# Edge network of a graph kernel: the table stands in the array and the one-hot moves, in two column tiles

## The chip, the cores and the metric

The kernel runs on one NeuronCore of one Trainium2 chip. Its engines are TensorE (PE: matmuls, with its weight loads shown as PEld), VectorE (DVE), ScalarE (ACT), GpSimd (POOL) and SyncE (SP, which here starts DMAs). The time of a run is the device time of the core in microseconds (us); the smaller the better.

## What is computed

Four graph layers run one after the other on 12500 nodes and 412500 edges (sorted by target). The change is in the third layer, a message passing network with 64 features and two rounds. Its edge part, cut to what matters:

```python
def _mlp(x, w0, b0, w1, b1):
    return silu(x @ w0 + b0) @ w1 + b1
...
for s in range(2):
    inp = concatenate([e, n[senders], n[receivers]], -1)
    upd_e = _ln(_mlp(inp, edge_blk_w0[s], edge_blk_b0[s], edge_blk_w1[s], edge_blk_b1[s]), ...)
    e = e + upd_e
    agg = segment_sum(upd_e or e, receivers, N)
    ...
```

The kernel multiplies each node's features by its share of edge_blk_w0 before the edges are visited, so the first layer of an edge is: a row picked from the sender table, plus a row picked from the receiver table, plus the edge's own state times its weights. The change is in how these rows are picked and added.

## The kernel before, in words

The two rounds are two edge passes, "first pass" (sorted_mlp with rnd 0, enc true, which also encodes the edge attributes) and "second pass" (rnd 1). In the trace both have tiles called e_s_...; the first pass lies at 8100 to 13790 us of the profiled execution, the second at 14200 to 18080.

The edges lie in 110 blocks of 35 cells of 128 slots. Cells 0 to 32 hold edges whose sender lies in a chunk of the table known beforehand (three chunks of 128 rows for each cell, all kept in SBUF as three bf16 parts in `parts`), cell 33 edges whose sender lies in the block's window, cell 34 the rest ("spill"), whose sender rows POOL fetches with an indirect DMA. Every cell also picks its receiver's row from the window. A block is worked in five groups of cells, PARTS5: 8, 8, 8, 8 and 3.

For each group and block:
- DVE `picks` (L1927, L1928) makes one-hots in bf16: `pick` (128 table rows by 128 slots for each chunk and cell) and `to_hot` for the window.
- PE `gather` (L2289 to L2294) loads a one-hot of 128 columns and moves 64 columns of the table through it, 9 matmuls a cell and 3 more for the window, into a bank `ps_g` with slots as partitions.
- DVE `gathered_` (L1944 to L1948) copies the bank to `g_sb` and adds the spill rows.
- PE `hidden1` (L2309) transposes `g_sb` by pairs of cells into the bank `ps_h1` (two cells of 64 features as partitions) and adds the edge state times weights there (L2312 in the first pass, L2315 in the second).
- ACT `act1_` (L2152) takes the bank through Silu; PE `out1` (L2322, L2325) is the second layer; ACT `out1_` (L2165, L2169) copies its result and squares it; DVE `var1` sums the squares.

Once a block DVE's `roots` (from L2036, twelve small steps) gives the standard deviations of both norms. Then `norm1` scales, and PE adds the messages up (`sums` L2352 in the first pass; `part0`, `less0`, `part1`, `part2` and `part_sums` L2341 in the second). The first pass also encodes the next block: `hidden0` (L2243), `act0_`, `out0` (L2250, L2253), `out0_` (copy and square), `var0`, `norm0` (L1935), and turns the states with `first_` (L2263) and `second_` (L2272). The attributes are turned by `attr_` (L2232).

Each engine has its own queue, written out by hand and strict in order; semaphores tie them. `body(k, x, before)` is one trip: it encodes block k, picks and computes block k - 1, and sums block k - 2, in steps s. On PE (L2364) a step of the first pass holds, in this order: first_(s-1), gather(s), hidden0(s), second_(s-1), sums(s-1), out0(s-1), hidden1(s-2), out1(s-3); after the steps comes carry. In the second pass: gather(s), part_sums(s-3), hidden1(s-2), out1(s-3). On ACT (L2182) a step holds: keep_first(s-2), keep_second(s-2), widens(s), part0(s-1), part1(s-2), first_(s-1), act0_(s), second_(s-1), out0_(s-1), act1_(s-2), out1_(s-3), each where the pass has it. DVE's body (L2039) ends with var0(4), windows, picks(0), picks(1) of the next block, the variances and roots.

In the first pass there is one bank each for ps_g, ps_h1 and ps_o1 (all eight banks are in use), in the second two of each. SP loads the states of a group after the hidden1 two groups back (L1860).

## Time and profile before

| | us |
|---|---|
| median of 3 runs (20420.85 to 20447.48) | 20424.32 |
| the profiled execution's own time | 20439.97 |
| its span, first to last instruction | 20438.1 |
| PE busy | 15983.6 (78%) |
| DVE busy | 13947.1 (68%) |
| ACT busy | 8065.7 (39%) |
| mean granted TensorE clock | 0.810 |

The busy time of each engine in 40 slices of 511 us shows the passes (each digit is tenths):

```profile
PE   2666667666668995999999999985999999966665
DVE  3777777777757995555454555545777777769999
ACT  1444444444432332555555555542333333321111
PEclk9555555655557996999999999997999999977676
```

Slices 16 to 27 are the first edge pass, 28 to 36 the second. In a timeline a row gives the start, the length to the end of the last instruction in it, the instructions merged, and in brackets how long the engine stood idle before it and for whom. Matmuls are pipelined: the time that one takes from the engine is from start to start, not its length. An f32 matmul runs as two records of two passes each. A row of the busy times of a stretch gives from and to, the length, the busy us (and instructions) of PE, PEld, DVE, ACT and POOL, the granted clock, the DMA share and GB/s. A row of a group by line gives line, engine, operation, out<-in, the shapes of the array and the operand, the count | busy us, mean ns of one | idle us of the engine before them and who ended it.

### The profile page before, as it was taken

To read this page: it belongs to the slowest core of one execution; us is meant where nothing else is said; L and a number is where in the kernel's file an instruction comes from. 1 tells how busy PE (TensorE), PEld (TensorE's weight loads), DVE (VectorE), ACT (ScalarE), POOL (GpSimd) and SP (SyncE) were. 2 spreads that over 40 slices of the span, in tenths; PEclk is the share of its full clock that TensorE was granted. 3 is DMA by queue.
4 is the path that set the end of the run, shared out by engine and by line. 5 is a ranking of instruction groups with operands and counts; after the bars stand their busy time and mean duration, and the time that the engine had idled before them with its cause. 6 is when DMAs were issued, how large, how long until landed. Compare 5 with 4: busy or idle time off the path is not lost. (4 is left out here: it accounts for less than half of the span.)

```text
span 20438.1 us, 578367 instructions
## 1 busy us (share of the span) xinstructions
PE 15983.6 (78%) x212634; PEld 14313.7 (70%) x212634; DVE 13947.1 (68%) x33417; ACT 8065.7 (39%) x17256; POOL 5201.9 (25%) x3993
## 2 busy tenths in 40 slices
PE   2666667666668995999999999985999999966665
PEld 1666666666656994888888888884777777756665
DVE  3777777777757995555454555545777777769999
ACT  1444444444432332555555555542333333321111
POOL 1888888888850110000000000000000000001111
PEclk9555555655557996999999999997999999977676
DMA  1222222222223551333333333322555555526666
GB/s 55 54 55 54 53 53 53 53 53 53 54 47 109 158 156 55 106 109 108 109 108 107 109 108 109 107 99 89 156 158 156 157 156 155 156 72 195 184 200 183
DMA packets 1482421, 2200.00 MB, mean 108 GB/s; under 512 B 773752, under 2 KB 960902, under 8 KB 1438482
## 3 DMA queue, kind: packets, MB, share of 16 engines
q1 hardware_dynamic: 1168298, 1839.20, 28.9%
q0 software_dynamic: 139040, 67.50, 3.8%
q10 hardware_dynamic: 173744, 272.32, 3.6%
q8 instruction: 1222, 20.02, 0.4%
q14 instruction: 117, 0.96, 0.0%
HBM read 1651.47 MB, written 523.16 MB: 106 GB/s over the span
## 5 line engine op out<-in xcount | busy, mean ns | idle before, releaser
L764 POOL DMA_INDIRECT records<-e_sort_rec,e_sort_index x3300 | 4339.2, 1315 | 1064.6 <-issue 990.2
L2289 PE MATMUL e_s_ps_g<-e_s_parts,e_s_pick 128*128 128x64 bf16 x65340 | 2900.2, 199 | 700.8 <-DVE e_s_to_hot L1928 336.8
L2289 PEld LDWEIGHTS e_s_ps_g<-e_s_parts,e_s_pick 128*128 128x128 bf16 x65340 | 2658.8, 102 | 849.6 <-issue 507.8
L2400 POOL DMA_INDIRECT e_s_spill<-send,e_s_lists x220 | 227.0, 1032 | 10094.0 <-DVE e_s_g_sb L1948 5471.4
L2294 PE MATMUL e_s_ps_g<-e_s_window,e_s_to_hot 128*128 128x64 bf16 x23100 | 1971.1, 199 | 0.0
L1944 DVE COPY e_s_g_sb<-e_s_ps_g 128x512 f32<-128x512 f32 x880 | 607.1, 690 | 1982.7 <-PE e_s_ps_h L2312 1376.6
L1093 PE MATMUL e_sort_acc<-e_sort_thirds,e_sort_hot 128*128 128x48 f32 x7260 | 1574.8, 414 | 318.6 <-DVE e_sort_hot L923 318.6
L1093 PEld LDWEIGHTS e_sort_acc<-e_sort_thirds,e_sort_hot 128*128 128x128 f32 x7260 | 1557.1, 332 | 351.0 <-DVE e_sort_hot L923 351.0
L2152 ACT ACTIVATE e_s_act<-e_s_ps_h,col_state 128x512 f32<-128x512 f32 (+1 forms) x1100 | 706.9, 643 | 1444.9 <-PE e_s_ps_h L2315 1390.3
L2294 PEld LDWEIGHTS e_s_ps_g<-e_s_window,e_s_to_hot 128*128 128x128 bf16 x23100 | 1263.6, 102 | 0.0
L1927 DVE TENSOR_SCALAR e_s_pick<-e_s_rows,lane_below 128x1024 bf16<-128x1024 bf16 (+1 forms) x3300 | 1244.6, 434 | 0.0
L2325 PEld LDWEIGHTS e_s_ps_o<-w_eblk,e_s_act 128*128 128x128 f32 x7920 | 1041.5, 192 | 259.1 <-issue 218.7
L1010 ACT ACTIVATE e_sort_away<-iota,e_sort_slots 128x128 f32<-128x128 f32 x3850 | 1171.0, 388 | 10.7
L1072 PE MATMUL e_sort_y<-e_sort_window,e_sort_turned 128*125 128x128 f32 x6600 | 1058.2, 330 | 58.0 <-DVE e_sort_prod L890 50.2
L1072 PEld LDWEIGHTS e_sort_y<-e_sort_window,e_sort_turned 128*125 128x125 f32 x6600 | 989.4, 236 | 115.0 <-DVE e_sort_prod L890 76.9
L2325 PE MATMUL e_s_ps_o<-w_eblk,e_s_act 128*128 128x128 f32 x7920 | 1061.7, 275 | 0.0
L1982 DVE TENSOR_REDUCE e_s_stat<-e_s_sq 128x8 f32<-128x512 f32 (+1 forms) x1100 | 652.6, 617 | 490.5 <-ACT e_s_sq L2169 490.4
L979 ACT ACTIVATE e_sort_turned<-e_sort_turn 128x500 f32<-128x500 f32 x880 | 493.7, 561 | 1181.1 <-PE e_sort_turn L1058 1023.8
L2352 PE MATMUL e_s_ps_sum<-e_s_unit,e_s_wide 128*128 128x128 f32 x7700 | 951.2, 275 | 0.1
L2315 PE MATMUL e_s_ps_h<-e_s_states,w_states 128*128 128x512 f32 x2200 | 941.2, 550 | 0.0
L1058 PE MATMUL e_sort_turn<-ident,e_sort_hot_d 125*128 125x125 bf16 x3300 | 502.7, 304 | 527.1 <-ACT e_sort_turned L979 449.4
L1344 PE MATMUL e_s_g<-e_s_parts,e_s_pick 128*128 128x48 bf16 x21780 | 815.2, 206 | 119.6 <-DVE e_s_pick_own L1240 64.4
(542 smaller groups left out, 35650.4 us busy)
## 6 DMA issues: line engine op xcount, KB each, us to landing
e_s_rows<-rows_d SPq DMA_DIRECT2D x330, 1088.0 KB, 5.3
e_s_hot<-hots_d SPq DMA_DIRECT2D x550, 560.0 KB, 4.1
e_s_states<-states SPq DMA_DIRECT2D x880, 256.0 KB, 3.7
e_s_to_rows<-rows_d SPq DMA_DIRECT2D x220, 608.0 KB, 6.0
e_s_rows<-rows_d SPq DMA_DIRECT2D x220, 544.0 KB, 4.9
e_s_rows<-rows_d SPq DMA_DIRECT2D x220, 512.0 KB, 5.5
e_s_to_rows<-rows_d SPq DMA_DIRECT2D x220, 512.0 KB, 6.5
states<-e_s_first_t ACTq DMA_DIRECT2D x440, 256.0 KB, 2.0
```

The lines of the kernel that those rows point to most:

```text
L764: pool.indirect_dma_start(records, bass.IndirectOffsetOnAxis(ap=index[x][:, t:t + 1], axis=0), rec[x][:, t, :], None,).then_inc(written[x] ...
L1010: last = act.activation(away[:, n - c, :], iota128[:, :], ACT.Square, scale=-1.0, bias=slots[x][:, n, 1:2])
L1072: mm = pe.matmul(ps_y[j % 2][0:P, (n - t) * AF:(n - t + 1) * AF], turned[x][:, n, :], window[x][:, :], start=True, stop=True)
L1093: mm = pe.matmul(acc[c // ACC][:, c % ACC * SPAN * F:(c % ACC + 1) * SPAN * F], hot[:, c, :], thirds[:, c, :, :].rearrange("p h f -> p (h ...
L1344: mm = pe.matmul(ps_g[g][:, at:at + 3 * F], pick[x][:, h, c * LANES:(c + 1) * LANES], parts[:, SPAN * c + h, :, :].rearrange("p r f -> p ( ...
L1927: dve.tensor_scalar(pick[p][:, h, 0:(f - c) * LANES], rows_[:, c * LANES:f * LANES], lane_below[:, h:h + 1], None, ALU.is_equal).then_inc( ...
L2152: act.activation(act1[p][:, 0:turned(s)], ps_h1[p % NB][:, 0:turned(s)], ACT.Silu, bias=(col_state if enc else col_state1)[:, :]).then_inc ...
L2289: pe.matmul(to_, pick[p][:, h, here], parts[:, SPAN * c + h, r, :], start=h == 0 and r == 0, stop=False)
L2294: mm = pe.matmul(to_, to_hot[p][:, here], window[:, r, 1, :], start=c == SPILL and r == 0, stop=r == 2)
L2315: mm = pe.matmul(ps_h1[p % NB][:, 0:n_], w_states1[r][:, :], states[p][:, r, 0:n_], start=False, stop=r == 1, skip_group_check=True)
L2325: mm = pe.matmul(ps_o1[p % NB][:, j * LANES:(j + 1) * LANES], act1[p][:, j * LANES:(j + 1) * LANES], W[f"eblk1{rnd}"][:, :], start=False, ...
L2352: mm = pe.matmul(ps_sum[:, 0:2 * D if enc else D], wide[s][:, (c - c0) * LANES:(c - c0 + 1) * LANES], units_of(x, c), start=c == 0, stop=F ...
```

## The change

The roles in the pick are swapped. The table part (128 rows by 64 columns) is loaded as the standing operand, and the one-hot (128 columns) moves. The result has features as partitions, which is the form that the first layer needs, so it goes straight into the bank `ps_h1`: cells of even place in the group into partitions 0 to 63, of odd place into 64 to 127, by two column tiles of the array of 64 columns each. Pick matmuls alternate between the two. The receiver rows of a group are picked with three matmuls for each half, of up to 512 columns. The spill rows are added in hidden1 by a matmul with the identity. The banks ps_g, the copies `gathered_`, the tile g_sb and the transposes are gone; ps_h1 has two banks in the first pass and five in the second. hidden1 comes one group after its gather, not two, and stands in a step right after hidden0; act1_, out1 and out1_ are one step earlier as well. gather waits for act1_ of the group that used its bank before (`aH`). POOL's spill DMA waits for hidden1 of two blocks before.

```diff
+        NH = 2 if enc else 5
...
-        ps_g, ps_h1, ps_o1, ps_sum = ps("g", NB), ps("h1", NB), ps("o1", NB), ps("sum")[0]
+        ps_h1, ps_o1, ps_sum = ps("h1", NH), ps("o1", NB), ps("sum")[0]
+
+        def hidden_bank(x, s):
+            return ps_h1[(x + s) % 2 if enc else s]
...
-            def gathered_(k, x, s, before):
-                p = (x + s) % 2
-                n_ = width(s)
-                dve.wait_ge(tg.sem, tg.at(f"{s}", k))
-                if s >= 2 or before:
-                    dve.wait_ge(tH.sem, group_at(tH, "", k, s, 2))
-                if s < NG - 1:
-                    dve.tensor_copy(g_sb[p][:, 0:n_], ps_g[p % NB][:, 0:n_]).then_inc(vg.sem, 1)
-                else:
-                    dve.tensor_copy(g_sb[p][:, 0:n_ - D], ps_g[p % NB][:, 0:n_ - D]).then_inc(vg.sem, 1)
-                    dve.wait_ge(spilled[x], block_of(k, x, 16))
-                    dve.tensor_tensor(g_sb[p][:, n_ - D:n_], ps_g[p % NB][:, n_ - D:n_], spill[x][:, :], ALU.add).then_inc(vg.sem, 1)
...
-                    if main and s:
-                        gathered_(k - 1, y, s - 1, before - 1)
...
-                act.activation(act1[p][:, 0:turned(s)], ps_h1[p % NB][:, 0:turned(s)], ACT.Silu, bias=(col_state if enc else col_state1)[:, :]).then_inc(aH.sem, 1)
+                act.activation(act1[p][:, 0:turned(s)], hidden_bank(x, s)[:, 0:turned(s)], ACT.Silu, bias=(col_state if enc else col_state1)[:, :]).then_inc(aH.sem, 1)
...
+                    if main and 1 <= s < NG + 1:
+                        act1_(k - 1, y, s - 1, before - 1)
                     if main and 2 <= s < NG + 2:
-                        act1_(k - 1, y, s - 2, before - 1)
-                    if main and s >= 3:
-                        out1_(k - 1, y, s - 3, before - 1)
+                        out1_(k - 1, y, s - 2, before - 1)
 
...
             def gather(k, x, s, before):
                 c0, e = PARTS5[s]
                 p = (x + s) % 2
+                halves = [hidden_bank(x, s)[half * D:(half + 1) * D, :] for half in range(2)]
                 pe.wait_ge(vp.sem, vp.at(f"to{s}", k))
                 if s == 0:
                     pe.wait_ge(vx.sem, vx.end(k))
-                if s >= NB or before:
-                    pe.wait_ge(vg.sem, group_at(vg, "", k, s, NB) if s >= NB or NB - s > 1 else vg.end(k - 1))
-                for c in range(c0, e):
-                    here = slice((c - c0) * LANES, (c - c0 + 1) * LANES)
-                    to_ = ps_g[p % NB][:, (c - c0) * D:(c - c0 + 1) * D]
-                    if c < OWN:
-                        for h in range(SPAN):
-                            for r in range(3):
-                                pe.matmul(to_, pick[p][:, h, here], parts[:, SPAN * c + h, r, :], start=h == 0 and r == 0, stop=False)
-                    elif c == OWN:
+                if s >= NH or before:
+                    pe.wait_ge(aH.sem, group_at(aH, "", k, s, NH))
+                to_pairs = to_hot[p][:, :].rearrange("p (j w l) -> p w j l", w=2, l=LANES)
+                for r in range(3):
+                    for half in range(2):
+                        n_ = (e - c0 + 1 - half) // 2
+                        pe.matmul(halves[half][:, 0:n_ * LANES], window[:, r, 1, :], to_pairs[:, half, 0:n_, :], start=r == 0, stop=False,
+                                  skip_group_check=True)
+                for j in pairs(s):
+                    mine = [(half, c0 + 2 * j + half) for half in range(2) if c0 + 2 * j + half < OWN]
+                    for h in range(SPAN):
                         for r in range(3):
-                            pe.matmul(to_, to_hot[p][:, here], window[:, r, 0, :], start=r == 0, stop=False)
+                            for half, c in mine:
+                                mm = pe.matmul(halves[half][:, j * LANES:(j + 1) * LANES], parts[:, SPAN * c + h, r, :],
+                                               pick[p][:, h, (c - c0) * LANES:(c - c0 + 1) * LANES], start=False, stop=False, skip_group_check=True)
+                if e > OWN:
+                    j, half = divmod(OWN - c0, 2)
                     for r in range(3):
-                        mm = pe.matmul(to_, to_hot[p][:, here], window[:, r, 1, :], start=c == SPILL and r == 0, stop=r == 2)
+                        mm = pe.matmul(halves[half][:, j * LANES:(j + 1) * LANES], window[:, r, 0, :], to_hot[p][:, (OWN - c0) * LANES:(OWN - c0 + 1) * LANES],
+                                       start=False, stop=False, skip_group_check=True)
                 mm.then_inc(tg.sem, 1)
 
             def hidden1(k, x, s, before):
-                p = (x + s) % 2
+                c0, p = PARTS5[s][0], (x + s) % 2
                 n_ = turned(s)
+                if s == NG - 1:
+                    j, half = divmod(SPILL - c0, 2)
+                    pe.wait_ge(spilled[x], block_of(k, x, 16))
+                    pe.matmul(hidden_bank(x, s)[half * D:(half + 1) * D, j * LANES:(j + 1) * LANES], spill[x][:, :], ident128[:, :], start=False, stop=False,
+                              skip_group_check=True)
                 if enc:
                     pe.wait_ge(au.sem, au.at(f"{s}", k))
+                    mm = pe.matmul(hidden_bank(x, s)[:, 0:n_], w_state[:, :], first_t[p][:, 0:n_], start=False, stop=True, skip_group_check=True)
                 else:
                     pe.wait_ge(states_in[p], groups_of(k, x, s, 0, 2))
-                pe.wait_ge(vg.sem, vg.at(f"{s}", k) if s < NG - 1 else vg.end(k))
-                if s >= NB or before:
-                    pe.wait_ge(aH.sem, group_at(aH, "", k, s, NB))
-                for j in pairs(s):
-                    f = min((j + 1) * 2 * D, width(s)) - j * 2 * D
-                    pe.matmul(ps_h1[p % NB][0:f, j * LANES:(j + 1) * LANES], g_sb[p][:, j * 2 * D:j * 2 * D + f], ident128[:, :], start=j == 0,
-                              stop=False, is_transpose=True, skip_group_check=True)
-                if enc:
-                    mm = pe.matmul(ps_h1[p % NB][:, 0:n_], w_state[:, :], first_t[p][:, 0:n_], start=False, stop=True, skip_group_check=True)
-                else:
                     for r in range(2):
-                        mm = pe.matmul(ps_h1[p % NB][:, 0:n_], w_states1[r][:, :], states[p][:, r, 0:n_], start=False, stop=r == 1, skip_group_check=True)
+                        mm = pe.matmul(hidden_bank(x, s)[:, 0:n_], w_states1[r][:, :], states[p][:, r, 0:n_], start=False, stop=r == 1, skip_group_check=True)
                 mm.then_inc(tH.sem, 1)
 
             def out1(k, x, s, before):
...
                         gather(k - 1, y, s, before - 1)
                     if new and s < NG:
                         hidden0(k, x, s, before)
+                    if main and 1 <= s < NG + 1:
+                        hidden1(k - 1, y, s - 1, before - 1)
                     if enc and out_ and 1 <= s < NG + 1:
                         second_(k - 2, x, s - 1, before - 2)
                     if enc and out_ and 1 <= s < NG + 1:
...
                     if new and 1 <= s < NG + 1:
                         out0(k, x, s - 1, before)
                     if main and 2 <= s < NG + 2:
-                        hidden1(k - 1, y, s - 2, before - 1)
-                    if main and s >= 3:
-                        out1(k - 1, y, s - 3, before - 1)
+                        out1(k - 1, y, s - 2, before - 1)
...
-                    pool.wait_ge(vg.sem, vg.end(k - 2))
+                    pool.wait_ge(tH.sem, tH.end(k - 2))
```

## Rows read from the trace of the kernel before

**Rows 1.** busy time of the engines in a stretch of each pass

```profile
8500.00:13500.00 5000.00, 4602.94 (x67563) 4214.43 (x67562) 2524.89 (x6592) 2583.30 (x4647) 90.52 (x96) 0.98 0.33 108
...
14300.00:17900.00 3600.00, 3290.81 (x53327) 2768.66 (x53327) 2645.31 (x6907) 1387.85 (x2532) 113.81 (x101) 0.94 0.51 156
```

**Rows 2.** groups by line, first pass, 8500 to 13500 us

```profile
L2289 PE MATMUL e_s_ps_g<-e_s_parts,e_s_pick 128*128 128x64 bf16 x28809 | 1258.2, 198 | 256.8 <-DVE e_s_g_sb L1944 249.9 <-issue 6.2
```

**Rows 3.** groups by line, second pass, 14300 to 17900 us

```profile
L2289 PE MATMUL e_s_ps_g<-e_s_parts,e_s_pick 128*128 128x64 bf16 x30213 | 1368.7, 201 | 308.1 <-DVE e_s_to_hot L1928 243.6 <-issue 64.5
```

**Rows 4.** timeline of PE, first pass: two cells one after the other

```profile
10005.97 0.43 PE L2289 MATMUL e_s_ps_g<-e_s_parts,e_s_pick 128*128 128x64 bf16 x9
...
10006.32 0.43 PE L2289 MATMUL e_s_ps_g<-e_s_parts,e_s_pick 128*128 128x64 bf16 x9
```

**Rows 5.** timeline of PE, first pass: hidden1 and first_; one out1

```profile
10027.73 0.60 PE L2309 MATMUL e_s_ps_h<-ident,e_s_g_sb 128*128 128x128 f32 x4
10028.16 1.02 PE L2312 MATMUL e_s_ps_h<-e_s_first_t,w_state 128*128 128x512 f32 x2
10029.02 0.60 PE L2263 MATMUL e_s_ps_u<-ident,e_s_unit 128*128 128x128 f32 x4
...
10038.45 0.38 PE L2322 MATMUL e_s_ps_o<-row_eblk,ones 128*128 128x512 bf16 x1
...
10039.56 0.60 PE L2263 MATMUL e_s_ps_u<-ident,e_s_unit 128*128 128x128 f32 x4
```

**Rows 6.** weight loads by shape, whole span

```profile
L2309 PEld LDWEIGHTS e_s_ps_h<-ident,e_s_g_sb 128*128 128x128 f32 x3740 | 440.9, 144 | 31.5 <-issue 29.4 <-DMA e_s_states<-states 1.9
L2309 PEld LDWEIGHTS e_s_ps_h<-ident,e_s_g_sb 128*64 128x64 f32 x220 | 24.2, 110 | 0.0
```

**Rows 7.** timeline of PE, second pass: a one-row matmul between others

```profile
16026.48 1.05 PE L2325 MATMUL e_s_ps_o<-w_eblk,e_s_act 128*128 128x128 f32 x8
16027.47 0.17 PE L2339 MATMUL e_s_ps_sum<-e_s_zeros 1*128 1x1 bf16 x1
16027.57 0.85 PE L2341 MATMUL e_s_ps_sum<-e_s_split,e_s_hot 128*128 128x193 bf16 x8
```

**Rows 8.** timeline of PE, first pass: first_(0), gather(1), after out0(4), first_(0)

```profile
10010.24 0.65 PE L2263 MATMUL e_s_ps_u<-ident,e_s_unit 128*128 128x128 f32 x4 [0.49 <-DVE e_s_unit L1935]
10013.07 0.44 PE L2289 MATMUL e_s_ps_g<-e_s_parts,e_s_pick 128*128 128x64 bf16 x9 [2.18 <-DVE e_s_g_sb L1944]
...
10048.79 0.60 PE L2309 MATMUL e_s_ps_h<-ident,e_s_g_sb 128*128 128x128 f32 x4
...
10060.45 0.66 PE L2263 MATMUL e_s_ps_u<-ident,e_s_unit 128*128 128x128 f32 x4 [0.41 <-DVE e_s_unit L1935]
```

**Rows 9.** timeline of ACT, first pass: out0_, act1_(0); square of group 4

```profile
10028.06 0.60 ACT L2116 ACTIVATE e_s_unit<-e_s_ps_o 128x512 f32<-128x512 f32 x1 [2.29 <-PE e_s_ps_o L2253]
...
10029.22 0.69 ACT L2152 ACTIVATE e_s_act<-e_s_ps_h,col_state 128x512 f32<-128x512 f32 x1
...
10050.08 0.36 ACT L2120 ACTIVATE e_s_sq<-e_s_unit 128x192 f32<-128x192 f32 x1
```

**Rows 10.** timeline of DVE, first pass: norm0(0) of the next trip

```profile
10059.70 0.69 DVE L1935 TENSOR_TENSOR e_s_unit<-e_s_unit,e_s_stat 128x512 f32<-128x512 f32 x1
```

**Rows 11.** timeline of PE, second pass: out1(4), gather(2), out1(1), next gather(2)

```profile
16604.56 0.61 PE L2325 MATMUL e_s_ps_o<-w_eblk,e_s_act 128*128 128x128 f32 x4
...
16614.08 0.66 PE L2289 MATMUL e_s_ps_g<-e_s_parts,e_s_pick 128*128 128x64 bf16 x9 [3.32 <-DVE e_s_to_hot L1928]
...
16632.40 1.05 PE L2325 MATMUL e_s_ps_o<-w_eblk,e_s_act 128*128 128x128 f32 x8
...
16650.21 0.62 PE L2289 MATMUL e_s_ps_g<-e_s_parts,e_s_pick 128*128 128x64 bf16 x9 [1.96 <-DVE e_s_to_hot L1928]
```

**Rows 12.** timeline of DVE, second pass: roots begin, copy of group 0

```profile
16643.01 0.20 DVE L2036 TENSOR_SCALAR e_s_stat<-e_s_stat 128x70 f32<-128x70 f32 x1
...
16647.80 0.69 DVE L1944 COPY e_s_g_sb<-e_s_ps_g 128x512 f32<-128x512 f32 x1
```

More of the change, by code:

```diff
@@ L1746, in sorted_mlp @@
         spill = tiles("spill", [LANES, D])
-        g_sb, act1 = tiles("g_sb", [LANES, 8 * D]), tiles("act1", [LANES, 512])
+        act1 = tiles("act1", [LANES, 512])
         sq1 = tiles("sq1", [LANES, 8 * D])
```

3 lines of the change are left out of this document (removed).

## Prediction

> **What bounds the kernel now.** I read the 40 slices first: the changed code runs only in the two edge network passes, where PE is the fullest engine. Then the groups by line and the busy times of one stretch of each pass. In the first pass PE is busy 4603 of 5000 us, in the second 3291 of 3600, at granted clocks of 0.98 and 0.94 (nearly all at 2.4 GHz) [rows 1]. A block has 297 picking matmuls (33 cells, 3 table chunks, 3 bf16 parts), so 28809 and 30213 of them are 97.0 and 101.7 blocks: 51.5 us and 35.4 us a block [rows 2, 3]. PE is busy but not alone in the loop. In the first pass it waits 249.9 us / 97 = 2.6 us a block for the DVE copy of the picked rows [rows 2]; in the second 243.6 / 101.7 = 2.4 us for the one-hot of group 2 [rows 3]. So I looked in the timelines for the ring each block must go round.
>
> First pass ring: first_(0) starts at 10010.24, the last out0 ends at 10048.79, and the next first_(0) starts at 10060.45 [rows 8]: 38.55 us on PE, then 11.65 us through ACT's square of group 4 (ends 10050.44 [rows 9]), DVE's windows, two one-hots, variances and roots, and norm0(0) [rows 10]. Square's end to first_(0) is 10.0 us of DVE work in one row. The period here is 50.2 us; the mean block has 1.3 us more.
>
> Second pass ring: gather(2) starts at 16614.08, out1(1) ends 0.9 us after 16632.40, the next gather(2) starts at 16650.21 [rows 11]: 19.2 us on PE, 16.9 us on ACT and DVE (part0(4), less0(4), windows, one-hots, roots from 16643.01, norm1, merge, the copy of group 0, one-hot 2 [rows 12]). A second way, from the end of out1(4) (16604.56 + 0.44) to gather(2) at 16614.08, is 9.1 us and nearly ties.
>
> **The change, part by part.** Picking. Today 12 load and matmul pairs of 64 moving columns take 10006.32 - 10005.97 = 0.35 us, 29.2 ns each [rows 4]; a full group of 8 cells has 96 of them, 2.8 us. The new form moves 128 one-hot columns against 64 table columns. The price of moved columns is in the f32 state matmul: 512 columns in four passes take 10029.02 - 10028.16 = 0.86 us, 215 ns a pass, so 0.42 ns a column and 54 to 56 ns for 128 [rows 5]. No row shows two column tiles at work. Bounds: side by side, a pair costs 56 ns; one after the other, 112 ns. I take 56, since the tiles share neither columns nor PSUM partitions, and weigh 84 and 112 as rivals. The load of 64 columns is no limit: 110 ns in length against 144 for 128 [rows 6], so about 0.5 ns a column, 34 ns for one, in the shadow of 54 to 56 ns of streaming, as today's loads are. A full group is then 36 pairs, 2.01 us, plus the window's three pairs of 512 columns, 0.65: 2.66 us, 0.14 less than now. Group 4 is 3 x 0.11 + 12 x 0.056 = 1.0 us against 0.7. Per block the picking comes out even (11.6 against 11.8).
>
> Change of array tiling. Before a group the array goes from 128x128 to two 128x64 tiles, and back. The nearest row is the one-row matmul L2339: the matmuls before it end their 0.89 us at 16027.37, it starts 0.10 later, and the next 0.10 after that, where a one-column step could be near nothing [rows 7]: about 0.1 us each way for bf16. With f32 behind it I take 0.24 for a round trip, five a block, 1.2 us; bounds 0 and 0.35 each (0 to 1.75). The Trainium skill, TensorEngine Tiling (Array Packing), Key Properties, says that changing the tiling mode drains TensorE; L2339 agrees with its 0.1 us each way. By a free change the sum below would be about 180 us lower.
>
> The turn of the picked rows goes: 0.43 us a group of 4 transposes (10028.16 - 10027.73 [rows 5]), 1.96 us a block. The spill row returns as one f32 matmul of 128 columns: 4 x 0.056 = 0.22 us, and 0.2 more for its own change of tiling. DVE loses four copies and two short ones, some 3.3 us a block (0.69 us each [rows 12]).
>
> Order. hidden1 moves from two groups behind to one, and stands ahead of second_, sums and out0; out1 moves from three to two. gather(s) waits for act1(s-2) in the first pass (two banks), for last block's act1 in the second (five banks). On ACT, act1_(s-1) is queued behind out0_(s-1), and that waits for PE's out0(s-1).
>
> First pass, leg on PE from first_(0) to out0(4), against 38.55:
> - waits for the copy: -2.6 [rows 2]. Transposes of three groups: -1.3. Five state matmuls in the leg, not three (out0(4) now stands behind hidden1(4)): +0.86 + 0.43 = +1.3. One more out1: 10039.56 - 10038.45 = +1.1 [rows 5, 8]. Gathers 1 to 4: -0.1, four changes of tiling +1.0. Spill +0.4.
> - new waits. gather(2) needs act1(0). From the end of PE's out0 to that of act1 is 10029.22 + 0.69 - 10027.73 = 2.2 us, 2.3 with the start [rows 5, 9], and PE has only first_(1), 0.44, meanwhile: +1.9. For gather(3) and gather(4) out1, 1.1, stands in between too: 2.3 - 1.55 = +0.75 each. hidden1(3) waits 0.65 for first_(3) on ACT, which is behind act1_(2), out1_(1) and a widening. hidden1(4) waits for ACT's first_(4), which is queued behind act1_(3) and out1_(2) (1.15 us): my walk has first_(4) done 2.3 us after PE is ready. Together +6.3, and second_(4), sums(4) and out0(4) are queued behind the last of these.
> Sum: -2.6 - 1.3 + 1.3 + 1.1 - 0.1 + 1.0 + 0.4 + 6.3 = +6.1, a leg of 44.6 us. The other leg is ACT's copy and square, 1.15 (ACT is idle then, where today it runs behind), and the same 10.0: 11.15. Ring: 55.8 against 50.2, +5.6; longer idle stretches should leave a little more at 1.2 GHz, +0.3 (0 to 1.5). +5.9 us x 110 blocks = +649 us. What hides the saved transposes and copies is thus this ring: PE gets 3 us of wait in front of first_(0).
>
> Second pass, same leg now from gather(2) to out1(2): gathers 2, 3, 4 (2.66 + 2.66 + 1.0), three changes 0.7, state matmuls of groups 1 to 3 (3 x 1.72), three out1 (3.3), part sums 0 and 1 (2.1): 17.6. Today's leg, up to out1(1), is 2.8 + 2.8 + 0.7 + 3 x 2.15 + 2.2 + 2.1 = 17.05 at full clock. The reason for one out1 more is ACT's queue: part0(4) stands behind out1_(2) now, behind out1_(1) before. ACT and DVE: 16.9 less one copy, 0.7: 16.2. The rest of today's period, 35.4 - 17.05 - 16.9 = 1.45, is clock and fetch: gather(2) runs 9 matmuls in 0.66 us after its wait where full speed gives 0.43 [rows 4, 11]. It stays, since PE still waits some 2.7 us there. Ring: 17.6 + 16.2 + 1.45 = 35.25, -0.15 us, -17 us in all (bounds: -0.6 by free changes of tiling, +0.6 by dear ones). The state loads now feed hidden1(0) two groups sooner; they land about 6 us into the block, just in time, and inside DVE's wait.
>
> Sum: 20440.0 (span 20438.1 and 1.9 around it) + 649 - 17 = 21072 us for a profiled execution; the median of the runs lies 15.7 below it, so 21056, rounded to **21050**. Tiling at its bounds, clock 0 to 1.5 us, half a wait more or less: 20750 to 21450.
>
> **Rivals.**
> - Faster: the waits don't form. PE runs at its own stream: the first pass loses 2.6 of wait and 0.6 of work (-3.2), the second falls to the 31.5 us that its PE work adds up to (-3.9), because DVE reaches its roots earlier than in my walk. -7.1 x 110: 19660; with the first pass alone 20090. It decides where ACT ends act1(0) within 0.5 us of out0(0), and first_(4) before out1(2). The 2.2 us of [rows 9] speak against it, DVE's freed 3.3 us for it.
> - Same: waits come out as long as today's, 20400 to 20480.
> - Half overlap: a pair costs 84 ns. +1.33 us a full group; first pass +9.7, second +1.0 (its wait fills): 21600.
> - The tiles don't overlap at all, so the change doesn't do what it says: 112 ns a pair, +2.66 us a full group, +0.17 the last. First pass 44.6 + 8.2 + 11.15 - 50.2 = +13.7, second PE-bound at 41.4 us, +6: 22600.
> - Loads are not hidden: each matmul costs 56 + 27 (64 columns at the 0.42 ns of streaming) = 83 ns, alone: 7.4 us a full group. +22.5 and +15.4 us a block: 24600. Today's loads hide under matmuls on the same rows [rows 4], which speaks against it. The Trainium skill, TensorE: Matmul & The Clock Gate, Part 3, has loads overlap a running matmul only where the row group differs, and all rows are in use here; the trace of before disagrees, with 29.2 ns for load and matmul of one row group.
>
> **How the numbers follow.** My forecast 0.50; half overlap 0.11; no overlap 0.14; loads exposed 0.02; faster 0.16; same 0.07. A measurement of this kernel tells about 0.2%, 41 us, from no change. Faster 0.16, same 0.07, slower 0.77. The range goes from 20100 (leaves out most of the faster case, 0.12) to 22650 (leaves out a little over 0.04).
>
> **What would show it.** Right: 36 pairs in 2.0 us; PE waiting for act1 ahead of gathers 2 to 4 in the first pass and for first_t ahead of hidden1(4); the wait before first_(0) near 3 us, from 0.5; 57 us a first-pass block, 35 a second. Wrong: starts of picking matmuls 56 ns apart (no overlap) or over 80 (loads); a second pass near 31.5 us a block; waits of PE for ACT under 1 us a block.

## The result, and the profile after

The changed kernel takes 20935.62 us (median of 4 runs, 20925.15 to 20957.02) against 20426.44 for the kernel before in the same session: ratio 1.0243, 95% interval 1.023 to 1.0256, 509 us slower. Forecast: 21050 us, slower.

| | us |
|---|---|
| span of the profiled execution | 20923.4 |
| PE busy | 15812.8 (76%) |
| DVE busy | 13286.2 (63%) |
| ACT busy | 8061.5 (39%) |
| mean granted TensorE clock | 0.816 |

The 40 slices, now of 523 us (rows of the page for the changed kernel, digits in tenths):

```profile
PE   2666666666668986888888888887699999966665
...
PEclk9565555565558987999999999998899999976776
```

The first edge pass has gone from nines to eights on PE, the second still reads nines. Next are the busy times of a stretch of each pass, and the group of the picking matmuls in the same two stretches (columns as in [rows 1, 2]).

```profile
8500.00:13500.00 5000.00, 4148.37 (x52156) 3571.14 (x52154) 1992.39 (x5334) 2310.11 (x4134) 81.19 (x86) 0.95 0.29 96
14900.00:17900.00 3000.00, 2736.45 (x39228) 2028.85 (x39225) 2081.78 (x5575) 1221.04 (x2254) 123.93 (x90) 1.00 0.52 165
```

```profile
L2281 PE MATMUL e_s_ps_h<-e_s_pick,e_s_parts 128*64 128x128 bf16 x25542 | 840.4, 222 | 41.5 <-issue 41.5
...
L2281 PE MATMUL e_s_ps_h<-e_s_pick,e_s_parts 128*64 128x128 bf16 x26883 | 850.0, 219 | 0.0
```

At 297 picks a block these are 86.0 blocks in 5000 us and 90.5 in 3000: **58.1 us a block in the first pass (before 51.5), 33.1 us in the second (before 35.4)** [rows 2, 3]. Over 110 blocks that is +725 and -247 us, together +478; the two spans differ by 485. Both passes moved, in opposite directions.

What PE waits for: the waits of PE, in total, times, longest, first pass and then second pass of the changed kernel.

```profile
PE e_s_ps_h L2300 <- ACT e_s_first_t L2114: 283.1, 172, 2.5
PE e_s_ps_h L2274 <- ACT e_s_act L2138: 252.1, 258, 1.7
PE e_s_ps_u L2249 <- DVE e_s_unit L1938: 198.7, 86, 2.7
PE e_s_ps_o L2311 <- ACT e_s_unit L2151: 59.5, 86, 0.7
```

```profile
PE e_s_ps_h L2304 <- DMA e_s_states<-states: 142.2, 89, 2.7
PE e_s_ps_sum L2328 <- DVE e_s_split L1962: 92.6, 89, 1.1
```

In the first pass PE is idle 9.9 us a block (5000 - 4148.4 over 86), before 4.1; its busy time grew by only 0.8 us (48.2 against 47.5). So of +6.6 us, 5.8 are waits. Three of them a block are for act1 (2.9 us) and two for first_t (3.3 us); before, PE waited 15.9 us in the whole stretch for act1, 0.2 a block, and nowhere for first_t. One block of the timeline of PE, changed kernel:

```profile
10034.66 0.65 PE L2249 MATMUL e_s_ps_u<-ident,e_s_unit 128*128 128x128 f32 x4 [2.03 <-DVE e_s_unit L1938]
...
10045.52 0.84 PE L2274 MATMUL e_s_ps_h<-e_s_to_hot,e_s_window 128*64 128x512 bf16 x6 [1.72 <-ACT e_s_act L2138]
10046.17 2.20 PE L2281 MATMUL e_s_ps_h<-e_s_pick,e_s_parts 128*64 128x128 bf16 x72
10048.30 1.16 PE L2229 MATMUL e_s_ps_h<-e_s_attr_t,w_pairs 128*128 128x128 f32 x8
...
10055.80 0.84 PE L2274 MATMUL e_s_ps_h<-e_s_to_hot,e_s_window 128*64 128x512 bf16 x6 [0.61 <-ACT e_s_act L2138]
...
10066.08 0.49 PE L2274 MATMUL e_s_ps_h<-e_s_to_hot,e_s_window 128*64 128x256 bf16 x6 [0.61 <-ACT e_s_act L2138]
...
10068.54 1.12 PE L2300 MATMUL e_s_ps_h<-e_s_first_t,w_state 128*128 128x512 f32 x2 [0.83 <-ACT e_s_first_t L2114]
...
10077.06 0.70 PE L2300 MATMUL e_s_ps_h<-e_s_first_t,w_state 128*128 128x256 f32 x2 [2.38 <-ACT e_s_first_t L2114]
...
10077.94 1.49 PE L2341 MATMUL e_s_ps_sum<-e_s_unit,e_s_wide 128*128 128x128 f32 x6
10079.22 0.42 PE L2236 MATMUL e_s_ps_o<-row_eenc,ones 128*128 128x256 bf16 x1
...
10080.28 0.63 PE L2311 MATMUL e_s_ps_o<-row_eblk,ones 128*128 128x512 bf16 x1
...
10091.48 1.11 PE L2249 MATMUL e_s_ps_u<-ident,e_s_unit 128*128 128x128 f32 x4 [2.69 <-DVE e_s_unit L1938]
```

Read from first_(0) at 10034.66 to the end of out0(4) at 10080.28: a leg of 45.6 us; from there through ACT and DVE to the next first_(0) at 10091.48: 11.2 us. The 72 picks of a full group take 10048.30 - 10046.17 = 2.13 us with the way out of the tiling. ACT's rows show what the 2.38 us wait is behind: first_(4)'s copy comes after out0_(3), act1_(3) and out1_(2).

```profile
10073.16 0.60 ACT L2102 ACTIVATE e_s_unit<-e_s_ps_o 128x512 f32<-128x512 f32 x1 [2.43 <-PE e_s_ps_o L2239]
10073.79 0.63 ACT L2106 ACTIVATE e_s_sq<-e_s_unit 128x512 f32<-128x512 f32 x1
10074.33 0.67 ACT L2138 ACTIVATE e_s_act<-e_s_ps_h,col_state 128x512 f32<-128x512 f32 x1
10074.90 0.59 ACT L2151 ACTIVATE e_s_unit<-e_s_ps_o 128x512 f32<-128x512 f32 x1
10075.52 0.63 ACT L2155 ACTIVATE e_s_sq<-e_s_unit 128x512 f32<-128x512 f32 x1
...
10076.62 0.38 ACT L2114 ACTIVATE e_s_first_t<-e_s_ps_u 128x256 f32<-128x256 f32 x1 [0.47 <-issue]
```

### The profile page after: what moved, and what is told of

The parts are those of the page before. It is cut to its first block and busy times, and to the rows that moved or that the text cites. A ratio compares the mean times of both kernels' runs of the same rounds, so it can differ in the third digit from the quotient of the medians.

```text
span 20923.4 us, 533871 instructions
## 1 busy us (share of the span) xinstructions
PE 15812.8 (76%) x192614; PEld 13548.9 (65%) x192614; DVE 13286.2 (63%) x32097; ACT 8061.5 (39%) x17256; POOL 5283.4 (25%) x3993
## 5 line engine op out<-in xcount | busy, mean ns | idle before, releaser
L1967 DVE TENSOR_REDUCE e_s_stat<-e_s_sq 128x8 f32<-128x512 f32 (+1 forms) x550 | 340.8, 620 | 3450.4 <-ACT e_s_sq L2106 3450.4
L2281 PEld LDWEIGHTS e_s_ps_h<-e_s_pick,e_s_parts 128*64 128x64 bf16 x65340 | 2061.6, 112 | 245.5 <-issue 91.5
L2281 PE MATMUL e_s_ps_h<-e_s_pick,e_s_parts 128*64 128x128 bf16 x65340 | 2117.3, 221 | 51.9 <-issue 51.9
L2274 PE MATMUL e_s_ps_h<-e_s_to_hot,e_s_window 128*64 128x512 bf16 (+2 forms) x6600 | 887.0, 372 | 434.8 <-ACT e_s_act L2138 320.4
L2304 PE MATMUL e_s_ps_h<-e_s_states,w_states 128*128 128x512 f32 x2200 | 1009.1, 581 | 171.4 <-DMA e_s_states<-states 171.4
L2341 PE MATMUL e_s_ps_sum<-e_s_unit,e_s_wide 128*128 128x128 f32 x7700 | 1020.0, 287 | 0.1
L1958 DVE TENSOR_TENSOR e_s_less<-e_s_unit,e_s_split 128x512 f32<-128x512 f32 (+1 forms) x550 | 341.8, 621 | 997.5 <-ACT e_s_split L2162 997.3
L2341 PEld LDWEIGHTS e_s_ps_sum<-e_s_unit,e_s_wide 128*128 128x128 f32 x7700 | 972.4, 204 | 0.4 <-issue 0.4
```

The costliest lines, as they stand in the source:

```text
L2274: pe.matmul(halves[half][:, 0:n_ * LANES], window[:, r, 1, :], to_pairs[:, half, 0:n_, :], start=r == 0, stop=False, skip_group_check=True)
L2281: mm = pe.matmul(halves[half][:, j * LANES:(j + 1) * LANES], parts[:, SPAN * c + h, r, :], pick[p][:, h, (c - c0) * LANES:(c - c0 + 1) * L ...
L2304: mm = pe.matmul(hidden_bank(x, s)[:, 0:n_], w_states1[r][:, :], states[p][:, r, 0:n_], start=False, stop=r == 1, skip_group_check=True)
L2341: mm = pe.matmul(ps_sum[:, 0:2 * D if enc else D], wide[s][:, (c - c0) * LANES:(c - c0 + 1) * LANES], units_of(x, c), start=c == 0, stop=F ...
```

## Experiments

The theory: in the first pass the new order of hidden1, act1 and out1 makes PE wait for ACT, and that is the whole loss; the tiled picking itself is no dearer, since two column tiles stream side by side; the second pass gains. The rivals: the loss is in the tiling (streams that overlap only in part, changes of tiling); or the second pass's gain is not of this change. Blocks are worked out as above, from the count of picks in 5000 us of the first pass and 3000 us of the second.

| kernel | median us | ratio to before (95%) | us a block, first | second (clock) |
|---|---|---|---|---|
| before | 20426 | 1 | 51.5 | 35.4 (0.94) |
| changed | 20936 | 1.0243 (1.023 to 1.0256) | 58.1 | 33.1 (1.00) |
| e1_second_only | 20179 | 0.9874 (0.9857 to 0.989) | 51.5 | 33.2 (0.99) |
| e2_order_only | 21653 | 1.06 (1.0582 to 1.0617) | 62.7 | 35.5 (0.98) |
| e3_act1_early | 20404 | 0.9988 (0.9978 to 0.9997) | 53.5 | 33.2 (0.99) |
| e4_hidden4_last | 20555 | 1.0061 (1.0044 to 1.0078) | 54.8 | 33.3 (0.99) |
| e5_both | 20213 | 0.9897 (0.9881 to 0.9914) | 51.8 | 33.2 (0.99) |
| e6_halves_apart | 21172 | 1.0365 (1.0348 to 1.0382) | 59.4 | 34.5 (1.00) |
| e7_states_first | 20873 | 1.022 (1.0203 to 1.0237) | 58.1 | 33.0 (1.00) |
| e8_widen_later | 20170 | 0.9881 (0.9864 to 0.9897) | 51.3 | 33.2 (0.99) |
| e9_halves_fully | 21917 | 1.0732 (1.0715 to 1.075) | 62.5 | 38.2 (1.00) |
| e10_all_moves | 20142 | 0.9863 (0.9846 to 0.9879) | 51.6 | 33.0 (1.00) |
| e11_longer_wait | 20997 | 1.028 (1.0263 to 1.0297) | 58.1 | 33.9 (0.99) |
| e12_pick2_first | 20319 | 0.995 (0.9933 to 0.9966) | 51.4 | 34.5 (0.94) |

**The two passes apart.** e1 keeps the function of the kernel before for the first pass and takes the new one for the second.

```diff
-                    sorted_way = sorted_mlp(sorted_st, name, rnd)
+                    sorted_way = (sorted_mlp_first if rnd == 0 else sorted_mlp_second)(sorted_st, name, rnd)
```

> First pass as before the change, second pass as after it. Theory (the loss is made in the first pass, the second pass gains): the second pass keeps its 33.2 us a block against 35.4 and its full clock, the first pass is back at 51.5 us a block, so the time is 20,426 less 2.2 us x 110 blocks = about 20,185 us. Rival (the column tiles and the mode changes cost time wherever they stand, the second pass's shorter block is only the trace's picture of a quiet stretch): not under 20,400 us. The second pass's granted clock should read 1.00 by the theory and 0.94 by the rival.

Measured 20179 us, forecast 20185: the changed second pass alone gains 247 us, and the trace's 2.2 x 110 is 242. Its clock reads 0.99, where the theory had 1.00 and the rival 0.94. It gains by itself, and the whole loss lies in the first pass.

**The order without the tiling.** e2 keeps the picks, the copies and the transposes of the kernel before, in both passes, and has only the order of the new one.

```diff
-                    if main and 2 <= s < NG + 2:
-                        act1_(k - 1, y, s - 2, before - 1)
-                    if main and s >= 3:
-                        out1_(k - 1, y, s - 3, before - 1)
+                    if main and 1 <= s < NG + 1:
+                        act1_(k - 1, y, s - 1, before - 1)
+                    if main and 2 <= s < NG + 2:
+                        out1_(k - 1, y, s - 2, before - 1)
```

(and the same shift of hidden1 and out1 on PE, with hidden1 right behind hidden0)

> Picks, DVE copies and transposes as before the change, in both passes; only the order is the new one (hidden layer and output of the second network one group earlier on PE, their activations one group earlier on ACT). Theory (the order makes the waits): in the first pass the gathers wait on act1_ (near 2.9 us a block) and hidden1 waits on first_t (near 3 us a block) although nothing is tiled, the block grows from 51.5 us to 57 to 60, the second pass stays within 1 us of 35.4, and the time is 21,000 to 21,400 us. Rival (the tiling makes the loss: mode changes, split loads, streams that overlap only in part): the order is free, the time stays within 100 us of 20,426.

Measured 21653 us, 250 us past the dear end of the expectation. The waits of PE in the first pass:

```profile
PE e_s_ps_h L2309 <- ACT e_s_first_t L2128: 406.1, 189, 3.1
PE e_s_ps_u L2263 <- DVE e_s_unit L1935: 214.3, 80, 2.9
PE e_s_ps_g L2289 <- DVE e_s_g_sb L1944: 166.8, 80, 2.3
```

In 79.7 blocks that is 5.1 us a block for first_t and 2.7 for first_(0), where the kernel before had none and 0.35 (34.1 us in 97 blocks), with 2.1 left of the copy's 2.6; the clock fell to 0.90, and PE's busy time a block grew by 4.1 us with it. The gathers' wait for act1, which I expected too, did not form: here the picks go to banks of their own. That part needs the new picking into the hidden layer's two banks. So the order costs 11.2 us a block, and going on from there to the changed kernel (tiled picks, no transposes, no copies) gives 4.6 back in the first pass and 2.4 in the second; the two kernels are 718 us apart. (In e2's second pass the clock rose to 0.98 as well, but PE waits there for the copy of the picked rows, 118.6 us in 84.5 blocks, and the block is no shorter.) So behind the same order the new picking, as a whole, is a gain; the loss comes with the order.

**ACT's queue.** e3 moves one activation.

```diff
                     if new and s < NG:
                         act0_(k, x, s, before)
+                    if enc and main and 1 <= s < NG + 1:
+                        act1_(k - 1, y, s - 1, before - 1)
...
-                    if main and 1 <= s < NG + 1:
+                    if not enc and main and 1 <= s < NG + 1:
                         act1_(k - 1, y, s - 1, before - 1)
```

> The changed kernel, but in the first pass ACT does act1_(s-1) right behind act0_(s) instead of behind out0_. Theory: the gathers' waits on act1_ (2.9 us a block) go, hidden1(4)'s wait on first_t shrinks only a little, the block falls from 58.1 to 54 to 55.5 us, the time from 20,936 to 20,480 to 20,650 us. Rival (the wait only moves: hidden0's results are late on ACT instead, or out0 waits, or the wait ahead of first_(0) grows by as much): the block stays over 57 us, the time over 20,850 us.

Measured 20404 us, 76 better than the good end. The act1 waits are gone (PE's largest are now first_t with 261.2 us / 93.5 = 2.8 and first_(0) with 2.0 a block), and the clock came up from 0.95 to 0.97, which the expectation had not counted: PE's busy time fell from 48.2 to 47.1 us a block.

**PE's queue.** e4 puts hidden1(4) behind out0(4), so that nothing on the way to DVE stands behind its wait.

```diff
-                    if main and 1 <= s < NG + 1:
+                    if main and 1 <= s < (NG if enc else NG + 1):
                         hidden1(k - 1, y, s - 1, before - 1)
...
+                    if enc and main and s == NG:
+                        hidden1(k - 1, y, NG - 1, before - 1)
```

> The changed kernel, but in the first pass PE does hidden1(4) behind out0(4) instead of ahead of it. Theory: out0(4) no longer stands behind the 2.4 us wait for first_t, DVE's norm0 chain starts that much earlier and the block falls by 2 to 3.5 us to 54.6 to 56.1, the time to 20,550 to 20,720 us. Rival (the ring is not set by the leg to out0(4), the wait is made up elsewhere): within 60 us of 20,936.

Measured 20555 us, block 54.8: as expected. e5 has both moves.

> The changed kernel with both moves in the first pass: act1_(s-1) behind act0_(s) on ACT, and hidden1(4) behind out0(4) on PE. Theory: e3_act1_early left a wait of 1.9 us for first_t(4) ahead of out0(4), and this move takes it off the leg, so the block falls from 53.5 us to 51.3 to 52.3 us and the time to 20,180 to 20,290 us; together the two moves give 640 to 750 us of the 936 less 20,426 plus what the second pass gained. Rival (the two moves mend the same microseconds): no better than the better of the two alone, 20,400 us within 40 us.

Measured 20213 us, block 51.8: as expected. The two moves together give 723 us, as much as the whole loss of the first pass, 725. So the loss came from where these two steps stand in the queues, and not from the tiled streams; but the waits for act1 could form only because the picks now go to the hidden layer's two banks (e2 has none of them). Nor does the new picking gain anything in the first pass: with both moves its block is 51.8 us, and it was 51.5 before. The two moves were not tried on the kernel before.

e8 also moves ACT's widening behind first_(s-1).

```diff
-                    if enc and out_ and s < NG:
-                        widens(k - 2, x, s)
...
                         first_(k - 1, y, s - 1, before - 1)
+                    if enc and out_ and s < NG:
+                        widens(k - 2, x, s)
```

> e5_both, and on ACT in the first pass widens(s) stands behind first_(s-1) instead of ahead of it. Theory: in e3_act1_early hidden1(3) still waited 0.96 us for first_t(3), which ACT made behind a widening of 0.5 to 1.06 us; that wait goes and the time falls by 0.7 to 1.1 us x 110, 80 to 120 us under e5_both's. Rival (widening is what the sums need, and they wait in its place, or the wait is made up ahead of first_(0)): within 40 us of e5_both.

Measured 20170 us, 43 better: half of what the theory expected and just over the rival's 40, and about as much as a measurement can't tell from nothing, so this move is not shown to gain. Of the 1.0 us, 0.2 came off first_t (139.7 us in 96.5 blocks, then 122.2 in 97.5): ACT's copy came sooner by less than the widening is long.

**Do two column tiles stream side by side?** e6 and e9 have the same 297 picks in another order: e6 nine picks of one half, then nine of the other; e9 all of one half, then all of the other.

```diff
-                    for h in range(SPAN):
-                        for r in range(3):
-                            for half, c in mine:
+                    for half, c in mine:
+                        for h in range(SPAN):
+                            for r in range(3):
```

> The changed kernel with the order of the picks inside a group turned: all picks of one column half, then all of the other, so that neighbours never sit in different column tiles. The same 297 matmuls a block. Theory (two column tiles stream side by side, a pair in 56 ns, and only neighbours of different halves do): one by one they take 53 to 60 ns each, 72 picks of a full group 3.8 to 4.3 us instead of 2.0, 8 us more a block in both passes; time 22,500 to 23,000 us. Rival (56 ns a pair is the rate of single matmuls whose loads are hidden, with no overlap of the streams): within 100 us of 20,936.

Measured 21172 us: the forecast of 22,500 was wrong, and so was the rival. In the trace the picks of one half start 55 to 56 ns apart, but around each change of half some of the other half's start between them: nine picks take 309 ns, 34 each. Started strictly in the queue's order, nine would take eight steps of 56 ns and one of 5, 453 ns; so PE reaches ahead over a few instructions. e9 leaves one such change in a group.

```diff
-                for j in pairs(s):
-                    mine = [(half, c0 + 2 * j + half) for half in range(2) if c0 + 2 * j + half < OWN]
-                    for h in range(SPAN):
-                        for r in range(3):
-                            for half, c in mine:
+                for half in range(2):
+                    for j in pairs(s):
+                        c = c0 + 2 * j + half
+                        for h in range(SPAN if c < OWN else 0):
+                            for r in range(3):
```

> The changed kernel with all picks of a group's first half ahead of all picks of its second, so that at most one crossing is left in a group where e6_halves_apart had one after every nine. e6 ran nine picks in 309 ns: some at 55 ns a matmul, some with matmuls of the other half slipping in, and cost 1.3 us a block in the second pass. Theory (PE streams two column tiles side by side, as far as the next few matmuls of its queue allow): now nearly every pick takes 55 to 56 ns, a full group's 72 take 3.7 to 4.0 us, the second pass's block grows from 33.1 to 39 to 42 us, the first pass's from 58.1 to 63 to 66 us; time 22,200 to 22,900 us. Rival (e6's 34 ns a pick is what any order without alternation costs): 21,170 us within 60 us.

Timeline of PE, second pass of e9, a full group and what follows it:

```profile
16606.60 3.99 PE L2281 MATMUL e_s_ps_h<-e_s_pick,e_s_parts 128*64 128x128 bf16 x72
16610.52 1.98 PE L2304 MATMUL e_s_ps_h<-e_s_states,w_states 128*128 128x512 f32 x4
```

16610.52 - 16606.60 = 3.92 us for 72 picks, where the alternating order takes 2.1. Singly, the picks of one half start 56 ns apart, 112 ns for two, and only around the one change of half do some start between others; with that change, 3.92 us are 109 ns for two. The column tiles do run side by side, and only when their matmuls are neighbours, or nearly so, in PE's queue. At 21917 us the whole was 280 under the expected range. In the second pass 5.0 of some 7.2 us (4 x 1.8) show: PE's waits shrank from 2.9 to 1.2 us a block (91.0 us in 78.6 blocks), since DVE went on beside the picks. The other 0.5 I can't place. In the first pass, 4.4 us show: gather(0) lies beside DVE's leg, and PE's wait for first_(0) shrank from 2.3 to 0.9 us a block (69.3 us in 80.0). The rest of the difference stays open.

**What holds the second pass.** e7 has SP issue the state loads first.

```diff
-                if mains(k, before):
-                    load_late(k - 1, 1 - x, before - 1)
                 if states_in_use:
                     load_states(k - 1, 1 - x, before - 1, (0, 1))
+                if mains(k, before):
+                    load_late(k - 1, 1 - x, before - 1)
```

> The changed kernel with SP issuing the second pass's state loads ahead of the late loads, instead of behind them (the first pass has no state loads). Theory (the second pass's ring is held by DVE, whose norm and splits come round every 33 us): PE's wait on e_s_states (1.6 us a block) goes and another of PE's waits, on to_hot or on the split, grows by the same; the time stays within 60 us of 20,936. Rival (PE's own chain is the ring): 1.2 to 1.6 us less a block, 20,760 to 20,800 us.

Waits of PE, second pass of e7:

```profile
PE e_s_ps_h L2274 <- DVE e_s_to_hot L1931: 153.7, 90, 1.8
PE e_s_ps_sum L2328 <- DVE e_s_split L1962: 93.6, 90, 1.1
```

The wait for the loads is gone (142.2 us in the same stretch) and 153.7 us of waiting for the one-hot, from 16.0, stands in its place: DVE's round is the ring, the wait only changed its name. The block is 0.2 us shorter, 21 us in all. The measured gain is 62, just past the theory's 60 and far from the rival's 136 to 176; the other 41 lie in neither stretch, and about as much is what a measurement can't tell from nothing. e10 is the sum of e8 and e7.

> e8_widen_later's first pass with e7_states_first's order of loads in the second pass. Theory (the two passes' gains are independent and add up): 20,170 less 62 = 20,110 us, within 30 us. Rival (with the first pass shorter the states lie in memory no earlier and the load order brings nothing): 20,170 us.

Measured 20142 us: 28 us under e8 and 32 over the theory's 20,110, so it lies between theory and rival and settles neither. The second pass is 0.24 us a block shorter than e8's, 26 us; the first pass, the same code as e8's, reads 51.6 against 51.3, 34 us the other way, so stretches of equal work lie that far apart. It is the fastest kernel here, 1.4% faster than the one before and 3.8% faster than the changed one.

**The clock of the second pass.** e11 adds an idle copy on DVE to e7, to bring back a wait as long as the old one.

```diff
...
+                if not enc and s == 2:
+                    dve.tensor_scalar(spare[:, :], rows_[:, 16 * LANES:33 * LANES], lane_below[:, 0:1], None, ALU.is_equal)
                 dve.tensor_scalar(to_hot[p][:, 0:(e - c) * LANES], to_rows[:, c * LANES:e * LANES], lane[:, 0:1], None, ALU.is_equal).then_inc(vp.sem, 1)
```

> e7_states_first with one idle copy of 2176 bf16 on DVE in the second pass, ahead of to_hot(2) (near 0.9 us, its result unused), so that PE's wait ahead of gather(2) goes from 1.8 to 2.7 us, near the 2.7 us that it was before the change. Theory (what the second pass gained beyond the forecast is the clock, which stays at full speed only while PE's longest wait stays short): the granted clock of the second pass falls from 1.00 to about 0.94 and the block grows by 0.9 us for the copy and by 1 to 1.7 us for the clock, 34.8 to 35.6 us; time 20,873 plus 210 to 290 us. Rival (the clock has another cause): the block grows by at most 0.9 us, the clock stays at 1.00, the time is at most 20,975 us.

The clock stayed at 0.99, the block grew by 0.98 us, where the copy itself takes 0.8, and the time is 20997 us. That is the rival's side, a little over its bounds (0.9 us, 1.00 and 20,975), and not the theory's 0.94 and 34.8 us. So a wait of 2.3 to 2.6 us in one piece did not lower the clock here. Three rows of a timeline of PE in e11:

```profile
16605.51 0.84 PE L2277 MATMUL e_s_ps_h<-e_s_to_hot,e_s_window 128*64 128x512 bf16 x6 [2.32 <-DVE e_s_to_hot L1934]
16606.18 2.18 PE L2284 MATMUL e_s_ps_h<-e_s_pick,e_s_parts 128*64 128x128 bf16 x72
...
16628.76 0.17 PE L2331 MATMUL e_s_ps_sum<-e_s_zeros 1*128 1x1 bf16 x1 [1.04 <-DVE e_s_split L1965]
```

After 2.32 us of idle PE is still at 2.4 GHz: 72 picks in 2.1 us. The block's other wait, 1.04 us, ends 23 us later, and the next 2.5 us one begins some 8 us after that. e12, made from e10, was meant to shorten both waits.

```diff
-                    if main and 1 <= s < NG - 1:
+                    if not enc and main and s == 0:
+                        picks(k - 1, y, 2, before - 1)
+                    if main and (1 if enc else 2) <= s < NG - 1:
                         picks(k - 1, y, s + 1, before - 1)
```

(and part2(4) ahead of the windows instead of behind picks(0))

> e10_all_moves, and in the second pass DVE makes the one-hots of group 2 ahead of norm1(0) and the merge instead of behind them, and the last split of the old block ahead of the new block's window casts and first one-hots. Theory (in e7 PE waited 1.8 us for to_hot(2) and 1.0 us for the last split, each only because DVE did other work first, and DVE sits idle for some 10 us later in the block): both waits shrink, the block falls from 33.0 to 30.5 to 31.8 us, the time by 130 to 270 us under e10_all_moves. Rival (DVE's round of norm, roots and splits is the ring, and what goes first in it only shifts the wait): within 60 us of e10_all_moves.

It made the second pass slower, by 1.5 us a block and 177 us in all, and neither theory had it. First DVE and then PE, second pass of e12:

```profile
15513.60 0.36 DVE L1962 TENSOR_TENSOR e_s_split<-e_s_less,e_s_split 128x192 bf16<-128x192 f32 x1 [2.20 <-ACT e_s_split L2168]
```

```profile
15514.01 0.17 PE L2332 MATMUL e_s_ps_sum<-e_s_zeros 1*128 1x1 bf16 x1 [0.56 <-DVE e_s_split L1962]
...
15516.83 1.49 PE L2278 MATMUL e_s_ps_h<-e_s_to_hot,e_s_window 128*64 128x512 bf16 x6 [2.29 <-DVE e_s_to_hot L1931]
15518.08 3.23 PE L2285 MATMUL e_s_ps_h<-e_s_pick,e_s_parts 128*64 128x128 bf16 x72
```

The last split, put first, needed ACT's part 2.2 us later, and all of DVE's windows and one-hots were queued behind it. PE's idle moved together: 0.56 and 2.29 us with half a microsecond of work between them, and the group after them partly at 1.2 GHz (window step 1.25 instead of 0.67 us, 72 picks up to the next row's start 3.05 instead of 2.1), granted clock of the pass 0.94. PE's waits are 2.8 us a block (246.7 us in 87.0 blocks), as in e10 (261.5 in 91.0, 2.9); what grew is its busy time, from 29.9 to 31.5 us. The kernel before has the same picture at 0.94; timeline of PE, second pass:

```profile
16504.11 0.23 PE L2289 MATMUL e_s_ps_g<-e_s_parts,e_s_pick 128*128 128x64 bf16 x2 [0.47 <-issue]
...
16506.69 0.50 PE L2289 MATMUL e_s_ps_g<-e_s_parts,e_s_pick 128*128 128x64 bf16 x9 [2.25 <-DVE e_s_to_hot L1928]
...
16507.15 0.67 PE L2289 MATMUL e_s_ps_g<-e_s_parts,e_s_pick 128*128 128x64 bf16 x9
```

In the changed kernel the two are 1.04 and 1.72 us, but 6 us of work lies between them, and the clock reads 1.00. In these four second passes two pieces of idle close together went with the lower clock, and about the same sum further apart, or in one piece, did not; but no run varied the distance alone. And the first pass of the changed kernel doesn't fit: there 0.83 us of idle, 6.1 us of work and the 2.38 us wait shown above are followed by a granted clock of 0.50 (10077.9 to 10080.3). What decides the clock stays open.

## Why the prediction was right, and where its sizes were off

**The picking: right.** 36 pairs were forecast at 56 ns, 2.01 us; a group's picks take 2.1 with the change of tiling, and e9 shows that the overlap is real and what it would cost without it. The rivals of half overlap (21600) and none (22600) fall. The price of no overlap was too high by half, though: e9 is 981 us above the changed kernel where that rival had some 1550. Two reasons show: waits took part of it up, and the rival also had the receiver picks of a group one after the other (0.65 us more a full group), which e9 leaves alternating, so e9 is not the whole of that case.

**The change of tiling: right.** I took 0.24 us a round trip. In the second pass of the changed kernel (rows below) out1's eight matmuls start at 16629.95 and the gather at 16630.94, 0.99 us, where [rows 5] have 1.11 less 0.21 for the bias matmul (16629.95 - 16629.74), 0.90: so 0.09 in; and 2.13 us for 36 pairs of 56 ns leaves 0.11 out. The Trainium skill, TensorEngine Tiling (Array Packing), Key Properties, says the mode change drains TensorE; this trace agrees in that the change costs time, 0.2 us a round trip, and shows no more of it.

**The new waits of the first pass: right, one by one.** Forecast, then read in the block shown above: gather(2) 1.9, read 1.72; gather(3) and (4) 0.75, read 0.61; hidden1(3) 0.65, read 0.83; hidden1(4) 2.3, read 2.38; before first_(0) near 3, read 2.0 to 2.7. The leg came out at 45.6 us against 44.6, the other leg at 11.2 against 11.15. The missing 1.0 us is the clock: behind the 2.38 us wait the sums and out0(4) run at half speed, with a granted clock of 0.50 (six sums take 10079.22 - 10077.94 = 1.28 us, where sixteen take 1.79 in the groups before). I had allowed 0.3 (0 to 1.5) for it. First pass: +649 forecast, +725 found.

**The second pass: the mechanism right, one term mis-sized.** The ring was forecast at 17.6 + 16.2 = 33.8 us and 1.45 of clock and fetch on top, kept from before because "PE still waits some 2.7 us there". Timeline of PE, second pass of the changed kernel:

```profile
16615.53 0.17 PE L2328 MATMUL e_s_ps_sum<-e_s_zeros 1*128 1x1 bf16 x1 [1.04 <-DVE e_s_split L1962]
...
16623.22 1.98 PE L2304 MATMUL e_s_ps_h<-e_s_states,w_states 128*128 128x512 f32 x4 [1.72 <-DMA e_s_states<-states]
16625.14 0.84 PE L2274 MATMUL e_s_ps_h<-e_s_to_hot,e_s_window 128*64 128x512 bf16 x6
...
16629.74 0.38 PE L2311 MATMUL e_s_ps_o<-row_eblk,ones 128*128 128x512 bf16 x1
16629.95 1.05 PE L2314 MATMUL e_s_ps_o<-w_eblk,e_s_act 128*128 128x128 f32 x8
16630.94 0.84 PE L2274 MATMUL e_s_ps_h<-e_s_to_hot,e_s_window 128*64 128x512 bf16 x6
...
16642.43 0.43 PE L2296 MATMUL e_s_ps_h<-ident,e_s_spill 128*64 128x128 f32 x2
```

From gather(2) at 16625.14 to the end of out1(2) at 16642.43 are 17.3 us (forecast 17.6), and the rest of a 33.1 us block is 15.8 (16.2). The 1.45 us is what did not stay: the idle of 2.7 us came back as two pieces in two places, and the clock kept its full speed. PE's idle a block is 2.9 us as before (3.0), its busy time fell from 32.4 to 30.2, and 32.4 x 0.94 is 30.4: by this count most of the gain of the pass is the clock. No run changed the clock alone. e12 against e10 speaks for it, with like waits, 0.94 in place of 1.00 and 1.5 us a block more; in e2 the clock rose to 0.98 and the block stayed, behind other waits. The state loads, forecast just in time, came late: PE waits 1.6 us a block for them (142.2 us in 90.5), and by e7 that costs 0.2. The forecast had -17 us in this pass and -247 were found. Against the forecast's 632 us over before, then, the first pass brings +76 and the second -230. That the two misses have opposite signs, and in part cancel in the total, is luck.

**The rival "faster, the waits don't form".** It put the point of decision rightly, at when ACT ends act1(0) and copies first_(4), and e3 and e5 are that case: with ACT's and PE's queues in another order the same picking gives 20213 us. It was priced at 19660 to 20090; its first-pass end of -3.2 us against the kernel before did not come, since PE still waits 4.8 us a block there (e5: 182.3 for first_(0), 139.7 for first_t and the rest of 461 us in 96.5 blocks).

## What to carry to other kernels

When a change moves a step on one engine closer to what feeds it, list what stands ahead of the feeding step in the other engine's queue: here one activation behind the wrong neighbour cost 4.7 us a block, and moving it and one PE step turned a kernel 2.4% slower than before into one 1% faster, with its gain in the second pass. A change that loses as a whole may hold a part that gains; running each pass with its own version (e1) found 250 us within one kernel. And before an instruction is put first in a queue, look whether its input is there: e12 put a split ahead that was not ready and lost 1.5 us a block where it was to save 1.2 to 2.5.

## What the runs showed of the hardware

- Two 128x64 column tiles of TensorE overlap fully when their matmuls alternate (56 ns for two matmuls of 128 bf16 columns, each with its own weight load), and not at all within long runs of one tile (112 ns for two, e9). With runs of nine they overlap in part, 34 ns a matmul where strict order would give 50: PE reaches a few instructions ahead (e6).
- Their weight loads stay hidden though all rows are in use. The Trainium skill, TensorE: Matmul & The Clock Gate, Part 3, has loads overlap a matmul in flight only where the row group differs; 56 ns a pair, with two loads of 110 ns in length, disagrees with that sentence. It fits another of the same part, by which a load into the background weight buffer is pulled ahead too.
- The granted clock did not follow the idle share: 2.7 us of idle a block in one place, broken once, read 0.94 (before; e12 with 2.85), nearly the same idle with 6 us of work between the two pieces read 1.00 (changed kernel), and 2.3 to 2.6 us in one piece read 0.99 (e11). In the first pass of the changed kernel a wait of 2.38 us, 6.1 us of work after one of 0.83, was followed by 0.50 all the same.
